# A mixture-of-experts tail: another order of broadcasts, biases and experts on TensorE

## The reference, cut to what matters

```python
t = t + _L1_ffn_ref(_ln_t(t), router_w, router_b, expert_w, expert_b)

def _L1_ffn_ref(x, router_w, router_b, expert_w, expert_b):     # D = C = 64, E = 8, K = 2
    router_probs = softmax(x @ router_w + router_b)
    top_p, top_i = top_k(router_probs, 2)
    top_p = top_p / sum(top_p)
    expert_out = einsum("bnd,edc->bnec", x, expert_w) + expert_b
    gathered = take_along_axis(expert_out, top_i[..., None], axis=2)
    return einsum("bnk,bnkc->bnc", top_p, gathered)
```

## Time and profile before

| | |
|---|---|
| time, median of 3 runs | 242.96 us (241.95 to 242.98) |
| time of the profiled execution | 242.9 us |
| span of the profiled execution | 241.1 us |
| TensorE busy | 231.1 us, 96% of the span |
| VectorE busy | 200.3 us, 83% |
| ScalarE busy | 172.6 us, 72% |
| GpSimd busy | 45.4 us, 19% |
| first gate broadcast to the start of the last additions | 225.85 to 237.99 us |

### The profile page before, as it was taken

One profiled execution on the slowest core, in us unless ns is written; L12 is line 12 of the kernel. 1 busy time (PEld: TensorE's weight loads), 2 busy tenths in 40 slices (PEclk: granted clock), 3 DMA queues, 4 the chain that ended last, 5 costly groups with the idle time before them and its releaser, 6 DMA issues.

```text
span 241.1 us, 6231 instructions
## 1 busy us (share of the span) xinstructions
PE 231.1 (96%) x2391; PEld 127.6 (53%) x2392; DVE 200.3 (83%) x425; ACT 172.6 (72%) x347; POOL 45.4 (19%) x80
## 2 busy tenths in 40 slices
PE   8899999999999999999999999999999998889894
PEld 6455455555554554555555555545444685558421
DVE  5799798999999999999999999999622683349773
ACT  3543739998999998999899998998996332329710
POOL 8946059500000000200000300030000000000250
PEclk9999999999999999999999999999999999999999
DMA  5005510061230211333300000000000000000002
GB/s 140 2 8 198 132 22 3 3 228 40 70 90 24 71 46 45 94 85 144 96 9 1 4 3 1 5 0 4 1 3 3 0 0 3 1 3 0 1 3 87
DMA packets 6082, 10.09 MB, mean 42 GB/s; under 512 B 2236, under 2 KB 3820, under 8 KB 5924
## 3 DMA queue, kind: packets, MB, share of 16 engines
q1 hardware_dynamic: 5908, 9.63, 13.3%
q10 hardware_dynamic: 144, 0.07, 0.1%
HBM read 6.84 MB, written 2.62 MB: 39 GB/s over the span
## 4 chain that ended last, share of the span: by engine, by line
PE 92%; DVE 3%; DMA 1%; ACT 1%; issue 1%; SPq 0%; DVEq 0%; ACTq 0%
PE psum L598 28%; PE psum L494 19%; PE psum L530 18%; PE psum L636 4%; PE psum L916 3%; PE psum L563 1%; PE psum L458 1%; PE psum L825 1%; PE psum L452 1%; PE psum L556 1%; DMA cols_sb<-in_cols 1%; PE psum L550 1%; PE psum L470 1%; PE psum L815 1%; PE psum L804 1%
## 5 line engine op out<-in xcount | busy, mean ns | idle before, releaser
L1305 DVE TENSOR_REDUCE half_max<-psum 128x1 f32<-128x512 f32 x256 | 156.1, 679 | 3.3 <-PE psum L494 3.0
L1123 ACT ACTIVATE probs<-psum 128x512 f32<-128x512 f32 x228 | 120.0, 601 | 14.6 <-PE psum L530 10.3
L494 PE MATMUL psum<-kop,qop 64*128 64x512 f32 x256 | 87.2, 443 | 0.7 <-DVE kop L1272 0.6
L530 PE MATMUL psum<-qop,kop 64*128 64x512 f32 x256 | 83.2, 441 | 0.5 <-ACT qop L1128 0.4
L598 PE MATMUL psum<-probs,v_aug 128*32 128x256 f32 (+1 forms) x1312 | 73.1, 339 | 0.2 <-DVE o_sb L1319 0.2
L494 PEld LDWEIGHTS psum<-kop,qop 64*128 64x128 f32 x256 | 40.5, 184 | 20.2 <-DVE half_max L1305 13.7
L530 PEld LDWEIGHTS psum<-qop,kop 64*128 64x128 f32 x256 | 39.4, 184 | 20.7 <-ACT probs L1123 11.2
L598 PEld LDWEIGHTS psum<-probs,v_aug 128*32 128x32 f32 x1312 | 32.7, 109 | 30.6 <-issue 20.7
L1016 POOL CAST max_part<-negmax 128x8 fp32r<-128x8 f32 x13 | 2.5, 190 | 92.5 <-issue 81.3
L1057 POOL TENSOR_TENSOR early<-probs,early 128x512 f32<-128x512 f32 x4 | 5.1, 1273 | 57.0 <-ACT probs L1217 56.9
L1119 ACT ACTIVATE probs<-psum 128x1024 f32<-128x1024 f32 x14 | 13.4, 1028 | 0.6 <-PE psum L530 0.4
(11 more groups left out here) (192 smaller groups left out, 200.8 us busy)
## 6 DMA issues: line engine op xcount, KB each, us to landing
parts_scratch<-early SPq DMA_DIRECT2D x4, 512.0 KB, 3.4
qop<-parts_scratch SPq DMA_DIRECT2D x28, 64.0 KB
vt_sb<-in_vt SPq DMA_DIRECT2D x1, 1024.0 KB, 4.8
kop<-parts_scratch SPq DMA_DIRECT2D x14, 64.0 KB
kop<-parts_scratch SPq DMA_DIRECT2D x28, 32.0 KB
x_sb<-in_x SPq DMA_DIRECT2D x2, 256.0 KB, 3.5
q_pair<-in_q_pairs SPq DMA_DIRECT2D x1, 512.0 KB, 3.7
qop<-max_row SPq DMA_DIRECT2D x26, 4.0 KB
```

The costliest lines, as they stand in the source:

```text
L494: last = nc.tensor.matmul(psum[:, m % MAX_BANKS, :], qop[at, b * PP + pp, qh * NH + t * P:qh * NH + (t + 1) * P], kop[at, b * PP + pp, c * ...
L530: last = nc.tensor.matmul(psum[:, bank, :], kop[at, b * PP + pp, mt * P:(mt + 1) * P], qop[at, b * PP + pp, qh * NH:(qh + 1) * NH], start= ...
L1123: last = nc.scalar.activation(probs[:, n % P_RING, h, :], psum[:, bank, :], ACT.Exp, scale=SCALE)
L1305: V.tensor_reduce(half_max[:, i, c, h * HT + t:h * HT + t + 1], psum[:, m % MAX_BANKS, :], AX_X, ALU.max, negate=True).then_inc(S["slot_fr ...
```

## The change

The three `keep_warm` products ahead of the gate transposes go. `experts` and `broadcasts` take a range of jobs and work through it pair by pair, each pair behind its own waits. The order becomes: broadcasts 0 to 3, first bias, broadcasts 4 and 5, second bias, experts 0 and 1, broadcasts 6 to 11, experts 2 to 7, broadcasts 12 to 15, experts 8 to 15. VectorE's addition for the first half moves behind its last product.

```diff
@@ tensor block
-            keep_warm(3, GB_BANKS[0])
             pe.wait_ge(S["logits_read"], 1)
...
-            def experts(first):
-                pair = range(first, first + B)
-                for r in pair:
...
+            def experts(first, end):
+                for pair in range(first, end, B):
+                    for r in range(pair, pair + B):
+                        if r in BY_DVE:
+                            pe.wait_ge(S["scaled_dve"], BY_DVE.index(r) + 1)
+                        else:
+                            pe.wait_ge(S["scaled_pool"], BY_POOL.index(r) + 1)
+                    for r in range(pair, pair + B):
+                        c, b, k = MOE[r]
+                        nc.tensor.matmul(psum[b * C:(b + 1) * C, MOE_BANKS[c], :], expw_sb[:, k, :],
+                                         scaled[:, r % SCALED, :], start=False, stop=k == E // 2 - 1,
+                                         skip_group_check=True).then_inc(S["moe_done"], 1)
             def broadcasts(first, end):
-                for i in range(first, end):
-                    gate_bank_free(i)
-                for i in range(first, end):
-                    gates_over_rows(i)
+                for pair in range(first, end, B):
+                    for i in range(pair, pair + B):
+                        gate_bank_free(i)
+                    for i in range(pair, pair + B):
+                        gates_over_rows(i)

             broadcasts(0, 4)
             expert_bias(0)
-            broadcasts(4, SCALED)
-            for first in range(0, len(MOE), B):
-                if first == len(MOE) // 2:
-                    expert_bias(1)
-                experts(first)
-                broadcasts(first + SCALED, min(first + SCALED + B, len(MOE)))
+            broadcasts(4, 6)
+            expert_bias(1)
+            experts(0, 2)
+            broadcasts(6, 12)
+            experts(2, 8)
+            broadcasts(12, 16)
+            experts(8, 16)
@@ vector block
                 V.tensor_tensor(scaled[:, i % SCALED, :], psum[:, GB_BANKS[i % len(GB_BANKS)], :],
                                 yt2[:, b, c * NH:(c + 1) * NH], ALU.mult).then_inc(S["scaled_dve"], 1)
-                if i == BY_DVE[-3]:
-                    dve.wait_ge(S["moe_done"], len(MOE) // 2)
-                    V.tensor_tensor(res[:, 0:NH], psum[:, MOE_BANKS[0], :], t2[:, 0:NH], ALU.add).then_inc(S["out_done"], 1)
+            dve.wait_ge(S["moe_done"], len(MOE) // 2)
+            V.tensor_tensor(res[:, 0:NH], psum[:, MOE_BANKS[0], :], t2[:, 0:NH], ALU.add).then_inc(S["out_done"], 1)
             dve.wait_ge(S["moe_done"], len(MOE))
```

## The result

The changed kernel takes 241.25 us (median of 20 runs, 240.54 to 247.84), the kernel before 242.97 (20 runs, 241.78 to 249.13). The ratio is 0.9929 with a 95% interval of 0.9902 to 0.9956, so 1.1 to 2.4 us less. I had forecast 241.7, with 1.25 us less. The profiled executions differ by more: spans of 241.1 and 238.8 us.

A forecast was written before the change was run, and what follows sets the result against it. TensorE, 92% of the last-ending chain, was taken to bound the kernel. Terms of 0.27, 0.25 and 0.75 us gave 1.27, written out 1.25 us less, so 241.7 us; 8-in-10 range 240.9 to 242.5.

The forecast's parts named there:

- Interruptions: TensorE's expert products broken off for broadcasts: 0.25 us each time; five become two, saving 0.75 us.
- The hole before the first experts: TensorE's 0.25 us wait for VectorE's second product, to be filled by the second bias; first experts 0.23 us later.
- The warming products: Three products ahead of the gate transposes, 0.32 us; leaving them out was to gain 0.27 us.
- Sum: All parts on TensorE's chain together: 1.25 us less.
- The thinnest margin: Before TensorE's last expert pair: VectorE's product 15 ready under 0.1 us before TensorE wants it.
- GpSimd's margin: GpSimd's products for jobs 8 and 11 ready 0.2 to 0.3 us before TensorE's last experts want them.
- rival A: Chain moves to VectorE or GpSimd, or transposes gain nothing; 0.3 to 0.6 us given back, 242.0 to 242.3; chance 0.20.
- The first output transfer: First half's output, issued at 236.1 instead of 235.05, lands at 238.1, before the end.
- The move of the addition: VectorE's first-half addition behind its last product, hidden by TensorE's last experts; at most 0.6 us cost if it delays VectorE.

The follow-up runs named there:

- group_only: Changed kernel with the three warming products back and the second bias back right before job 8; 242.90 us, ratio 0.9983 against the kernel before.
- bias_addlate: Kernel before with the second bias ahead of the first experts and the first half's addition behind VectorE's last product; 243.57 us, ratio 1.0020.
- add_inside: Changed kernel with the first half's addition back between VectorE's products 13 and 14; 241.67 us, ratio 0.9962 against the kernel before.
- order_warm: Changed kernel with the three warming products put back; 241.50 us, ratio 0.9956 against the kernel before.
- no_warm_54: Changed kernel without the 44 and 10 warming products ahead of the two groups of y transposes; 242.28 us, ratio 0.9981 against the kernel before.
- warm_only: Kernel before with only the three warming products left out; 242.63 us, ratio 1.0000.
- warm_pairwait: Kernel before without the three warming products and with broadcasts waiting pair by pair; 241.95 us, ratio 0.9970.
- one_break: Changed kernel with ten slots for scaled rows instead of six and one interruption of the experts fewer; 240.75 us, ratio 0.9932 against the kernel before.

## Why the prediction was right

The mechanism, the terms and the sign held. Point by point:

- Interruptions: 3 x 0.25 = 0.75 forecast, 0.73 measured in group_only.
- The hole before the first experts: 0.25 forecast; 0.25 measured (bias_addlate). The first experts start 4.20 us behind the y transposes, against 4.02 before; forecast was 0.23 later, measured 0.18.
- The warming products: 0.27 forecast, 0.33 measured. The term was undersized: I had let VectorE's split of the gates hold the transposes for 0.05 us, and they followed at once, 0.93 behind (1.25 less 0.32).
- Sum: 1.25 forecast, 1.30 measured; alone and with their companions the parts give 0.33 + 0.25 + 0.73 = 1.31.
- The thinnest margin: I had product 15 end 11.76 us behind the y transposes. It ended at 11.73 (234.38), and the load of the last pair is indeed released by it, but the sixteen products go on without a gap:

```profile
234.29 0.68 DVE L1530 TENSOR_TENSOR early<-psum,probs 128x512 f32<-128x512 f32 x1
234.49 0.23 PEld L915 LDWEIGHTS psum<-early,expw_sb 128*64 128x64 f32 x4 [0.70 <-DVE early L1527]
235.00 1.94 SPq L428 DMA_DIRECT2D out<-early  x3
```

- GpSimd's margin, the other one of rival A: its product for job 11 ended 9.83 us behind the y transposes (forecast 9.91), and the experts that need it start near 10.14 behind. It held.
- The first output transfer goes out at 235.00, 12.35 behind the y transposes (forecast 12.41), and its 256 KB hold nobody up: the last additions are followed by 3.15 us to the end of the span, 3.11 before.

What the working left out: it priced the parts as if each stood for itself. Two pieces of the change have no price in the sum, and the others fall short without them. The move of the addition, booked at nothing although the margin of product 15 was worked out with it, carries 0.47 us, and the pairwise waits, which I had used silently when I let broadcasts 0 and 1 start ahead of ScalarE's fourth copy, carry 0.19. Without the first a third of the gain would be missing (add_inside), without the second a seventh, as measured in the old order.

The forecast of the whole time was right in its range and 0.45 us above the median. The trace gives 1.30 us for the change; the medians differ by 1.72. The difference lies within the interval of the ratio, and two chances of 1 us and more per execution are shown to be there (the last section); that they make up just these 0.4 us is not shown. So it is the stage, 1.30 us against 1.25, that tests the working; the whole time carries these chances on top.

## What to carry to other kernels

When an engine fills the chain, price its changes of kind between groups of instructions, not only the instructions: here going from expert products to broadcasts and back cost 0.25 us each time even with all data ready. A part that brings nothing alone can be worth its full price once the wait behind it is gone (0 and 0.25 us for the same move of a bias), so look at which engine released the next instruction before the part is dropped. And for gains under 1% measure a distance between two instructions of the trace around the change: it repeated within 0.01 us in two profiles of the same kernel, where the whole time spread by more than the gain.

## What the runs showed of the hardware

- When TensorE reaches full speed at the start of an execution is a matter of chance at the scale of these gains. The 30 idle products of 128 bf16 columns ahead of L452 take 3.38 us in the profiles of before and after, 0.11 us each, twice the 0.056 us of the gate transposes (eight in 0.61, with 0.22 for the last), which have as many columns. So they ran at half the rate, 1.2 GHz by their spacing, although the views give the granted clock as 1.00 there. The clock's own record in the trace begins later, with the rise to 1.00: at 6.71 to 6.79 us in the three profiles (before, order_warm, bias_addlate) in which the two products of L452 take 2.07 or 2.08 us, and at 3.67 to 5.11 us in the nine others, where they take 1.12 to 1.28 us in eight and 1.45 in one (no_warm_54, 5.11). In add_inside, with the earliest rise, the last four idle products already start 0.056 us apart. What follows moves along: the second y transposes start at 223.69 to 223.82 in the three, and at 222.56 to 223.06 in the six others whose clock did not fall later and that have all warming products ahead of them. What decides the moment of the rise stays open.
- The clock can also fall for a while in code that is the same in all kernels, with TensorE at work: from 24.2 to 31.0 us in add_inside and from 24.6 to 41.7 in warm_only it was 0.50, though TensorE had been busy for 0.92 us or more of each microsecond from 12 us on, as in the profile of the changed kernel, where the clock stayed at 1.00. The second y transposes then start 3 and 7 us later. Why it fell in these executions stays open.
- In a stretch without TensorE work from 215.9 to 220.7 us the granted clock fell to 0.50 near its end, at 220.2, and it was back at 227.0 (no_warm_54). Leaving out the three warming products in front of work that came anyway changed nothing in the clock (1.00 throughout in warm_pairwait and both profiles of the changed kernel).
- Weight loads of 128-row products start while earlier products with the same rows still run (in one_break a load at 230.95, while products that start 0.43 us apart go on without a gap, 24 in 5.35 us). This goes against the list in the Trainium skill's "TensorE: Matmul & The Clock Gate", section "The mechanism", that lets them only where the row groups differ; the sentence above that list, which also allows a background weight buffer, would fit.
